# Cross-attention and FP4 feed-forward on one core: a step's small job put ahead of its maxima, rows' second half some steps later, another prologue

## The chip, the cores and the metric

The kernel runs on one core of one Trainium2 chip. The metric is the device time of one execution in microseconds (us). Engines are named as the profile does: PE (TensorE, its weight loads as PEld), DVE (VectorE), ACT (ScalarE), POOL (GpSimd) and SP (SyncE, which here only issues DMAs).

## The reference, cut to what matters

```python
# x: (8, 512, 256), ctx: (8, 1601, 256), 16 heads of 16
x = x + attention(layernorm(x), ctx, ctx)        # Wq, Wk, Wv, Wo with biases, softmax over 1601 keys
h = layernorm(x)
# fp4_quant_dequant: blocks of 16 along the last axis; scale = max|x| / 6; values to the grid 0, .5, 1, 1.5, 2, 3, 4, 6
gate = fp4(h) @ fp4(w_gate).T                    # 704 wide
up   = fp4(h) @ fp4(w_up).T
x = x + fp4(silu(gate) * up) @ fp4(w_down).T
```

## The kernel before, in words

The eight batches go through a software pipeline: a prologue ("pre"), then iterations "first", six times "loop", "last", and a "tail". An iteration computes the attention of one batch (part "att") and, in the same steps, the projections of the next batch ("early"), the feed-forward of the batch before ("late"), in "first" the rounding and transposing of the feed-forward weights ("once"), and the layernorm of the batch after the next ("next").

An iteration has 52 steps: 4 groups of 4 heads, 13 key tiles each. In a step PE computes two scores tiles (L811, `scores(n, 0)`), a job in a shared PSUM bank ("side 0": a piece of a projection, of gate, up or down), two more scores tiles, two products from which DVE takes row maxima for a later softmax (L828, `pair_products`; DVE reads them at L1082 and L1084), where the step has one a second, small job ("side 1"), and the weighted sum of the step before (L843). ACT takes the exponentials (L1007) and copies most jobs out of PSUM. All order is written out by hand: `SLOTS` says which jobs a step has on either side, `DVE_EXTRA` and `POOL_WORK` what DVE and POOL do besides.

In the loop all jobs use one bank, `misc`, in turn. So `shared(job)` first makes PE wait until the job before it was read. For a job of side 1 this is the job of side 0 in the same step: gate is read by ACT (tanh, L953) and DVE (L1111), up by DVE (L1116), a key piece by ACT (L938, L939), a value piece by ACT together with a context tile (L943, L919). Jobs of side 1 are transposes: `nm` (the maxima, L721), `hqT` (the hidden rows, L749), `xqT 1` (the second half of the rows, L732), and in "first" `ctx2` (context tiles, L681).

The rows that enter gate and up are rounded to FP4 in two halves: `xscale`, `xpower` and `xlast` on DVE, `xround` on POOL between the last two, then `xqT` on PE. The weights' pieces in "first" go through `W_AMAX_AT`, `W_SCALE_AT`, `W_SCALED_AT`, `W_POWER_AT`, `W_ROUND_AT` (steps on DVE and POOL) and end in `wT` (transposes on PE, two for each of six pieces; L768, L771). ACT loads the next piece after every second `wT`.

In the prologue `first_queries` has ACT issue the DMAs of the first group's queries and keys; then ACT waits until these have landed and issues the loads of the remaining weights (`weights_in`, L884 to L887). PE's sixth and seventh key pieces and the second query block (L692, L706) share three banks.

The side 1 transposes and the order that the change touches, in PE's loop over the steps:

```python
for job in products[between:2]:
    pair_products(job)
for job in jobs(it, n, 1):
    shared(job)
if n and has_att:
    weighted(n - 1, "att")
```

Of the kernel before, what the change touches and what calls it, by code (L numbers as in the profile page):

```python
# [12 lines left out]
I = 704  # L13
# [32 lines left out]
BLOCKS = 6 * 16  # L46
# [43 lines left out]
    16: ([("k", 5, "early")], []),  # L90
    17: ([("k", 6, "early")], []),
    18: ([("k", 7, "early")], []),
    19: ([("xqT", 0, "late")], [("xqT", 1, "late")]),
    20: ([("gate", 0, "late"), ("bob", 0, "once")], []),
    21: ([("gate", 1, "late"), ("wT", 0, "once")], [("nm", 2, "att")]),
    22: ([("up", 0, "late"), ("wT", 1, "once")], []),
    23: ([("up", 1, "late")], []),
    24: ([("gate", 2, "late"), ("wT", 2, "once")], []),
    25: ([("gate", 3, "late"), ("wT", 3, "once")], []),
    26: ([("up", 2, "late")], []),  # L100
    27: ([("up", 3, "late")], [("hqT", 0, "late")]),
    28: ([("gate", 4, "late")], [("hqT", 1, "late")]),
    29: ([("down0", 0, "late")], []),
    30: ([("down", 0, "late"), ("wT", 4, "once")], []),
    31: ([("gate", 5, "late"), ("wT", 5, "once")], []),
    32: ([("up", 4, "late")], [("hqT", 2, "late")]),
    33: ([("up", 5, "late")], [("hqT", 3, "late")]),
    34: ([("gate", 6, "late")], [("nm", 3, "att")]),
    35: ([("down0", 1, "late"), ("wT", 6, "once")], []),
    36: ([("down", 1, "late"), ("wT", 7, "once")], []),  # L110
    37: ([("gate", 7, "late")], [("hqT", 4, "late")]),
    38: ([("up", 6, "late")], [("hqT", 5, "late")]),
    39: ([("up", 7, "late")], []),
    40: ([("down0", 2, "late"), ("wT", 8, "once")], []),
# [43 lines left out]
for _step in SLOTS.values():  # L158
# [8 lines left out]
DVE_EXTRA = {  # L167
    2: [("late", "values", 4)], 3: [("late", "values", 5)], 4: [("late", "values", 6)], 5: [("late", "values", 7), ("late", "stats", 0)],
    7: [("late", "stats", 1), ("late", "mean", 0)], 8: [("late", "root", 0)], 9: [("late", "apply", 0)], 10: [("att", "nm", 1)],
    11: [("late", "xscale", 0)], 12: [("late", "xpower", 0)], 13: [("late", "apply", 1)], 14: [("late", "xscale", 1)], 15: [("late", "xpower", 1)],  # L170
    16: [("late", "xlast", 0)], 17: [("late", "xlast", 1)],
    21: [("att", "nm", 2)], 23: [("late", "hscale", 0)], 24: [("late", "hpower", 0)], 27: [("late", "hscale", 1)], 28: [("late", "hpower", 1)],
    29: [("att", "values", 0)], 30: [("att", "values", 1)], 32: [("att", "values", 2)], 33: [("late", "hscale", 2)], 34: [("late", "hpower", 2)], 36: [("att", "nm", 3)], 38: [("att", "values", 3)], 39: [("late", "hscale", 3)], 40: [("late", "hpower", 3)],
    43: [("next", "stats", 0)], 44: [("next", "stats", 1)], 45: [("next", "mean", 0)], 46: [("next", "root", 0)],
# [1 line left out]
}  # L176
PRE_EXTRA = {
    1: [("early", "stats", 0), ("early", "stats", 1), ("early", "mean", 0), ("early", "root", 0), ("early", "apply", 0), ("early", "apply", 1)],
    12: [("next", "stats", 0), ("next", "stats", 1)], 13: [("next", "mean", 0), ("next", "root", 0)], 14: [("next", "apply", 0), ("next", "apply", 1)],
    47: [("early", "nm", 0)],  # L180
}

TAIL_EXTRA = {
# [6 lines left out]
EXTRAS = {"pre": PRE_EXTRA, "first": DVE_EXTRA, "loop": DVE_EXTRA, "last": DVE_EXTRA, "tail": TAIL_EXTRA}  # L190


W_AMAX_AT = {12: 0, 14: 1, 24: 2, 27: 3, 33: 4, 39: 5}
W_SCALE_AT = {13: 0, 15: 1, 25: 2, 28: 3, 34: 4, 40: 5}
W_POWER_AT = {17: 0, 20: 1, 26: 2, 31: 3, 37: 4, 42: 5}
W_SCALED_AT = {14: 0, 16: 1, 25: 2, 28: 3, 34: 4, 40: 5}
W_ROUND_AT = {18: 0, 20: 1, 26: 2, 31: 3, 37: 4, 42: 5}
POOL_WORK = {
    0: [("late", "bias", 0)], 10: [("early", "k", 0)], 11: [("early", "k", 1)], 12: [("early", "q", 0), ("early", "k", 2)], 13: [("early", "k", 3)],
    14: [("late", "xround", 0), ("early", "k", 4)], 16: [("early", "q", 1), ("late", "xround", 1)], 17: [("early", "k", 5)], 18: [("early", "k", 6)], 19: [("early", "k", 7)],  # L200
    24: [("late", "hscaled", 0)], 25: [("late", "hround", 0)], 28: [("late", "hscaled", 1)], 29: [("late", "hround", 1)],
    34: [("late", "hscaled", 2)], 35: [("late", "hround", 2)], 40: [("late", "hscaled", 3)], 41: [("late", "hround", 3)],
}
# [68 lines left out]
def xattn_ffn(nc, x, ctx_in, wqT, wkT, wvT, woT, bq, bk, bv, bo, w_gate, w_up, w_down, out, scr_k, scr_q):  # L272
    es = ExitStack()
    with es:
# [38 lines left out]
        att = sb("att", [128, NC2, S])  # L313
# [5 lines left out]
        ht = sb("ht", [128, QT, I])  # L319

        mt = sb("mt", [128, QT * E])
        xnT = mt[:, :].rearrange("p (c n) -> p c n", c=NC2)
        hqT = sb("hqT", [128, NF, 128])
# [37 lines left out]
        k_stack = [[sem(f"k_stack{g}_{n}") for n in ("lead", "rest")] for g in range(NG)]  # L361
        q_stack = [[sem(f"q_stack{g}_{n}") for n in ("lead", "rest")] for g in range(NG)]
# [21 lines left out]
        def jobs(it, n, side):  # L384
            return [j for j in slots(it.kind, n)[side] if j[2] in it.parts]
# [28 lines left out]
        def maxima(it, n):  # L414

            part, first, number = ("early", 2 * (n - STEPS + M_LEAD), 2) if n >= STEPS - M_LEAD else ("att", 2 * (n + M_LEAD), 2)
            if it.kind == "first" and n < CATCH_UP:
                first, number = M_GROUP + AHEAD + 3 * n, 3
            if it.kind == "pre":

                first, last = (first, M_GROUP) if n < STEPS - M_LEAD + M_HEADS else (first - 2, M_GROUP + AHEAD)
                if not (n != STEPS - M_LEAD + M_HEADS and first < last):
                    return []
            if part not in it.parts:
                return []
            found = []
            for q in range(first, first + number):
                g, j = divmod(q, M_GROUP)
                pair, piece = divmod(j, M_HEADS)
                found.append((part, q, g, j, 2 * pair, piece))  # L430
            return found
# [4 lines left out]

        def rows_rounding(it, k):

            return mt[:, 0:512] if it.kind == "tail" else ht[:, :, :].rearrange("p t n -> p (t n)")[:, 512 * k:512 * (k + 1)]

        def raw_piece(p):

# [188 lines left out]
        def _(pe):  # L631
# [7 lines left out]
            def body(it):  # L639
# [209 lines left out]
                for n in range(STEPS):  # L849
                    if has_att:  # L850
                        scores(n, 0)
                    for job in jobs(it, n, 0):
                        shared(job)
                    products = maxima(it, n)

                    between = 1 if has_att and not jobs(it, n, 0) else 0
                    for job in products[:between]:
                        pair_products(job)
                    if has_att:
                        scores(n, 1)  # L860
                    for job in products[between:2]:
                        pair_products(job)
                    for job in jobs(it, n, 1):
                        shared(job)
                    if n and has_att:
                        weighted(n - 1, "att")
                    elif n == 0 and has_late:
                        weighted(STEPS - 1, "late")
                    for job in products[2:]:
                        pair_products(job)  # L870
# [3 lines left out]
        def _(act):  # L874
# [22 lines left out]
            def body(it):  # L897
# [123 lines left out]
                for n in range(STEPS):  # L1021
                    if has_att:
                        exps(n, 0)
                    for job in jobs(it, n, 0):
                        take(job)
                    if it.kind == "pre" and n == 14:
                        first_queries()
                        act.wait_ge(q_stack[0][1], BLOCKS)
                        act.wait_ge(k_stack[0][1], BLOCKS)
                        weights_in()  # L1030
                    if it.kind == "first" and n == 4:
                        raw_in(0)
                        raw_in(1)
                    if has_att:
                        exps(n, 1)
                    for job in jobs(it, n, 1):
                        take(job)
                    if n == 0 and has_late:
                        group_out(NG - 1, "late")
                    elif n and n % NKT == 0 and has_att:  # L1040
                        group_out(n // NKT - 1, "att")
# [4 lines left out]
        def _(dve):  # L1046
# [13 lines left out]
            def body(it):  # L1060
# [213 lines left out]
                for n in range(STEPS):  # L1274
                    for job in jobs(it, n, 0):
                        take(job)
                    if it.kind == "pre" and n == 11:
                        for piece in range(4):
                            first_keys(piece)
                    todo = maxima(it, n)  # L1280
                    for job in todo:
                        maximum(job)
                    for job in jobs(it, n, 1):
                        take(job)
                    if it.kind == "first":
                        if n in W_AMAX_AT:
                            weight_maxima(W_AMAX_AT[n])
                        if n in W_SCALE_AT:
                            weight_scales(W_SCALE_AT[n])
                        if n in W_POWER_AT:  # L1290
                            weight_powers(W_POWER_AT[n])
                    for part, what, k in EXTRAS[it.kind].get(n, []):
                        if part in it.parts:
                            extra(part, what, k)
# [5 lines left out]
        def _(pool):  # L1300
# [43 lines left out]
            def body(it):  # L1344
# [63 lines left out]
                for n in range(STEPS):  # L1408
# [10 lines left out]
                    if it.kind == "first":  # L1419
                        if n in W_SCALED_AT:  # L1420
                            weight_scaled(W_SCALED_AT[n])
# [31 lines left out]
```

## Time and profile before

| | |
|---|---|
| time, median of 3 runs (lowest, highest) | 1744.49 us (1743.31, 1746.17) |
| the profiled execution's own time | 1745.13 us |
| its span, first to last instruction | 1743.3 us |
| busy, share of the span: PE, DVE, ACT, POOL | 95%, 82%, 65%, 32% |
| mean granted TensorE clock, share of 2.4 GHz | 0.984 |

A timeline row gives start, duration, engine, line and operation, what is written and read, and in brackets how long the engine had been idle before it and what ended that. Consecutive groups of matmuls overlap a little in these rows, since their ends are modelled. Where a releaser named in brackets had ended long before, it was another that ended last.

### The profile page before, as it was taken

To read this page: it belongs to the slowest core of one execution; us is meant where nothing else is said; L and a number is where in the kernel's file an instruction comes from. 1 tells how busy PE (TensorE), PEld (TensorE's weight loads), DVE (VectorE), ACT (ScalarE), POOL (GpSimd) and SP (SyncE) were. 2 spreads that over 40 slices of the span, in tenths; PEclk is the share of its full clock that TensorE was granted. 3 is DMA by queue.
4 is the path that set the end of the run, shared out by engine and by line. 5 is a ranking of instruction groups with operands and counts; after the bars stand their busy time and mean duration, and the time that the engine had idled before them with its cause. 6 is when DMAs were issued, how large, how long until landed. Compare 5 with 4: busy or idle time off the path is not lost.

```text
span 1743.3 us, 26971 instructions
## 1 busy us (share of the span) xinstructions
PE 1648.1 (95%) x9408; PEld 656.0 (38%) x9408; DVE 1428.3 (82%) x2077; ACT 1131.4 (65%) x2293; POOL 564.2 (32%) x673
## 2 busy tenths in 40 slices
PE   5799899999999999999999999999999999989958
PEld 2332234333433344333443334333443334323325
DVE  6777988988788978988889887889879887889347
ACT  2377677766777667776677667776677766666731
POOL 4328520732025330443107321263304431013304
PEclk8899999999999999999999999999999999999979
DMA  5645332331234333142323322244222322200000
GB/s 162 145 85 123 88 69 44 85 105 38 56 58 107 83 60 57 51 112 48 78 45 83 102 41 58 46 117 85 58 54 54 77 47 66 44 7 10 13 22 13
DMA packets 106770, 117.52 MB, mean 67 GB/s; under 512 B 23236, under 2 KB 88140, under 8 KB 106636
## 3 DMA queue, kind: packets, MB, share of 16 engines
q1 hardware_dynamic: 101808, 111.62, 30.0%
q10 hardware_dynamic: 4828, 4.18, 1.0%
q8 instruction: 75, 1.23, 0.3%
q14 instruction: 59, 0.48, 0.1%
HBM read 76.78 MB, written 30.16 MB: 61 GB/s over the span
## 4 chain that ended last, share of the span: by engine, by line
PE 74%; DVE 15%; ACT 4%; POOL 3%; issue 2%; DMA 1%; SPq 1%; ACTq 0%; POOLq 0%; DVEq 0%
PE pvb L843 19%; PE st L811 18%; PE mx L828 9%; PE misc L741 7%; DVE cmx L1082 7%; PE misc L713 5%; PE misc L706 3%; PE misc L761 3%; ACT prob L1007 3%; PE misc L753 2%; PE misc L692 1%; PE misc L727 1%; PE misc L749 1%; POOL ht L1333 1%; PE misc L782 1%
## 5 line engine op out<-in xcount | busy, mean ns | idle before, releaser
L1007 ACT ACTIVATE prob<-st 128x512 f32<-128x512 f32 (+1 forms) x1590 | 867.2, 599 | 378.7 <-PE st L811 376.2
L1082 DVE TENSOR_REDUCE cmx<-mx 128x2 f32<-128x1024 f32 x768 | 905.8, 1220 | 156.4 <-PE mx L828 153.0
L811 PE MATMUL st<-qstack,kstack 112*128 112x512 bf16 (+1 forms) x1590 | 497.0, 385 | 9.9 <-ACT prob L1007 4.2
L843 PE MATMUL pvb<-prob,vv 128*32 128x512 f32 (+1 forms) x3328 | 444.7, 606 | 0.5 <-ACT prob L1007 0.5
L811 PEld LDWEIGHTS st<-qstack,kstack 112*128 112x128 bf16 (+1 forms) x1590 | 127.6, 98 | 463.4 <-issue 239.9
L828 PE MATMUL mx<-kstack,qstack 48*128 48x512 bf16 (+1 forms) x2048 | 257.9, 338 | 31.1 <-DVE cmx L1082 22.6
L1341 POOL TENSOR_TENSOR ht<-ht,rh 128x352 f32<-128x352 f32 (+1 forms) x78 | 56.8, 751 | 439.2 <-DVE rh L1058 439.2
L741 PE MATMUL misc<-wguT,rowsT 128*128 128x352 f32 x456 | 153.7, 459 | 0.0
L1333 POOL TENSOR_TENSOR ht<-ht,mt 128x352 f32<-128x352 f32 (+1 forms) x140 | 124.4, 911 | 73.5 <-DVE mt L1239 60.8
L828 PEld LDWEIGHTS mx<-kstack,qstack 48*128 48x128 bf16 x2048 | 59.4, 94 | 214.6 <-issue 131.7
L1347 POOL TENSOR_TENSOR cin<-cin 128x400 f32<-128x400 f32 (+1 forms) x60 | 55.8, 931 | 239.2 <-ACT cin L939 239.2
L843 PEld LDWEIGHTS pvb<-prob,vv 128*32 128x32 f32 (+1 forms) x3328 | 65.7, 108 | 133.4 <-issue 121.5
L1364 POOL TENSOR_TENSOR x<-x,bob 128x256 f32<-128x256 f32 x32 | 22.3, 729 | 287.0 <-issue 270.9
L741 PEld LDWEIGHTS misc<-wguT,rowsT 128*128 128x128 f32 x456 | 86.5, 190 | 40.9
L713 PE MATMUL misc<-wv,ctxT 128*128 128x256 f32 (+1 forms) x392 | 101.8, 382 | 0.0
L706 PE MATMUL misc<-ctxT,wk 128*128 128x400 f32 (+1 forms) x236 | 91.5, 510 | 0.0
L713 PEld LDWEIGHTS misc<-wv,ctxT 128*128 128x128 f32 (+1 forms) x392 | 73.1, 187 | 21.2 <-issue 0.5
L1144 DVE RECIPROCAL sums<-sums 128x128 f32<-128x128 f32 x64 | 60.3, 942 | 17.7 <-DMA sums<-pvs 17.7
L1341 POOL TENSOR_TENSOR ht<-ht,sh 128x352 f32<-128x352 f32 (+1 forms) x82 | 62.4, 783 | 2.9
L1333 POOL TENSOR_TENSOR xa<-xa,ht 128x256 f32<-128x256 f32 x56 | 43.1, 790 | 54.9 <-DVE ht L1196 53.8
L1351 POOL TENSOR_TENSOR cin<-cin 128x400 bf16<-128x400 f32 (+1 forms) x60 | 58.2, 970 | 4.7
L938 ACT ACTIVATE cin<-misc,bqk 128x400 f32<-128x400 f32 (+1 forms) x59 | 35.1, 595 | 32.8 <-PE misc L706 30.5
(182 smaller groups left out, 1542.0 us busy)
## 6 DMA issues: line engine op xcount, KB each, us to landing
kstack<-scr_k SPq DMA_DIRECT2D x378, 100.1 KB, 4.3
scr_k<-cin SPq DMA_DIRECT2D x48, 300.0 KB, 3.9
qstack<-scr_q SPq DMA_DIRECT2D x372, 32.0 KB, 1.8
cin<-ctx_in SPq DMA_DIRECT2D x16, 512.0 KB, 5.3
scr_q<-qp SPq DMA_DIRECT2D x16, 384.0 KB, 4.2
scr_k<-cin SPq DMA_DIRECT2D x16, 300.8 KB, 4.9
xn<-x SPq DMA_DIRECT2D x8, 512.0 KB, 3.9
cin<-ctx_in SPq DMA_DIRECT2D x16, 256.0 KB, 5.4
```

The costliest lines, as they stand in the source:

```text
L706: last = mm(o[:, 0:w], wk[:, h, m * 128:(m + 1) * 128], ctxT[:, h, COFF[n]:COFF[n] + w], start=(h == 0), stop=(h == NC2 - 1))
L713: last = mm(o[0:w, 0:E], ctxT[:, h, KOFF[j]:KOFF[j] + w], wv[:, h, :], start=(h == 0), stop=(h == NC2 - 1))
L741: last = mm(o[:, 0:IH], rowsT[:, h, t * 128:(t + 1) * 128], wguT[:, h, first:first + IH], start=(h == 0), stop=(h == NC2 - 1))
L811: mm(score_bank(it, n, h)[0:KROWS[kt], :], kstack[:, hd, KOFF[kt]:KOFF[kt] + KROWS[kt]], qstack[:, hd, :], start=True, stop=True).then_inc ...
L828: last = mm(mx[:, q % 2, par, at:at + w], qstack[r0:r0 + LEAD, hd, t * 128:(t + 1) * 128], kstack[r0:r0 + LEAD, hd, k0:k0 + w], start=True ...
L843: last = mm(pvb[2 * D * h:2 * D * (h + 1), :], vv[0:w, kt, (HG * g + h) // 2, D * (h % 2):D * (h % 2 + 2)], prob[0:w, n % 2, h, :], start= ...
L1007: activate(prob[0:KROWS[kt], n % 2, 2 * pair + h, :], score_bank(it, n, 2 * pair + h)[0:KROWS[kt], :], ACT.Exp, scale=SCALE).then_inc(exp_ ...
L1082: v.tensor_reduce(cmx[:, g % 2, h0:h0 + 2, at:at + 1], products, op=ALU.max, axis=AX.X).then_inc(max_free, 1)
L1144: v.reciprocal(sums[:, cols], sums[:, cols]).then_inc(rec_ready, 1)
L1333: last = g_.tensor_tensor(out[:, cols], in0[:, cols], in1[:, cols], op)
L1341: last = g_.tensor_tensor(part, part, over(sc[:, j * w:(j + 1) * w]), ALU.mult)
L1351: g_.tensor_tensor(parts[:, 2, :], whole, parts[:, 1, :], ALU.subtract).then_inc(done, 1)
```

## The change

The second half of the rows moves back: `xscale 1` from step 14 to 15, `xpower 1` from 15 to 17, `xlast 1` from 17 to 20, `xround 1` on POOL from step 16 (ahead of key pieces 5 and 6) to 18 (behind them), `xqT 1` from step 19 to 22; its scratch lies at another place in `ht`. In "first", `wT` 0 to 7 and most of their preparation come a step or two later. In the prologue half of a layernorm's last operation goes from step 14 to 50, and ACT no longer waits for the stacks before `weights_in`, which goes to step 36. On PE a step's side 1 job is put ahead of its products, and on DVE the side 1 job ahead of the maxima.

```diff
-    19: ([("xqT", 0, "late")], [("xqT", 1, "late")]),
+    19: ([("xqT", 0, "late")], []),
-    21: ([("gate", 1, "late"), ("wT", 0, "once")], [("nm", 2, "att")]),
-    22: ([("up", 0, "late"), ("wT", 1, "once")], []),
-    23: ([("up", 1, "late")], []),
-    24: ([("gate", 2, "late"), ("wT", 2, "once")], []),
-    25: ([("gate", 3, "late"), ("wT", 3, "once")], []),
-    26: ([("up", 2, "late")], []),
+    21: ([("gate", 1, "late")], [("nm", 2, "att")]),
+    22: ([("up", 0, "late"), ("wT", 0, "once")], [("xqT", 1, "late")]),
+    23: ([("up", 1, "late"), ("wT", 1, "once")], []),
+    24: ([("gate", 2, "late")], []),
+    25: ([("gate", 3, "late"), ("wT", 2, "once")], []),
+    26: ([("up", 2, "late"), ("wT", 3, "once")], []),
...
-    30: ([("down", 0, "late"), ("wT", 4, "once")], []),
-    31: ([("gate", 5, "late"), ("wT", 5, "once")], []),
-    32: ([("up", 4, "late")], [("hqT", 2, "late")]),
+    30: ([("down", 0, "late")], []),
+    31: ([("gate", 5, "late"), ("wT", 4, "once")], []),
+    32: ([("up", 4, "late"), ("wT", 5, "once")], [("hqT", 2, "late")]),
...
-    35: ([("down0", 1, "late"), ("wT", 6, "once")], []),
-    36: ([("down", 1, "late"), ("wT", 7, "once")], []),
-    37: ([("gate", 7, "late")], [("hqT", 4, "late")]),
+    35: ([("down0", 1, "late")], []),
+    36: ([("down", 1, "late"), ("wT", 6, "once")], []),
+    37: ([("gate", 7, "late"), ("wT", 7, "once")], [("hqT", 4, "late")]),
...
-    11: [("late", "xscale", 0)], 12: [("late", "xpower", 0)], 13: [("late", "apply", 1)], 14: [("late", "xscale", 1)], 15: [("late", "xpower", 1)],
-    16: [("late", "xlast", 0)], 17: [("late", "xlast", 1)],
+    11: [("late", "xscale", 0)], 12: [("late", "xpower", 0)], 13: [("late", "apply", 1)], 15: [("late", "xscale", 1)], 16: [("late", "xlast", 0)],
+    17: [("late", "xpower", 1)], 20: [("late", "xlast", 1)],
...
-    12: [("next", "stats", 0), ("next", "stats", 1)], 13: [("next", "mean", 0), ("next", "root", 0)], 14: [("next", "apply", 0), ("next", "apply", 1)],
-    47: [("early", "nm", 0)],
+    12: [("next", "stats", 0), ("next", "stats", 1)], 13: [("next", "mean", 0), ("next", "root", 0)], 14: [("next", "apply", 0)],
+    47: [("early", "nm", 0)], 50: [("next", "apply", 1)],
...
-W_AMAX_AT = {12: 0, 14: 1, 24: 2, 27: 3, 33: 4, 39: 5}
-W_SCALE_AT = {13: 0, 15: 1, 25: 2, 28: 3, 34: 4, 40: 5}
-W_POWER_AT = {17: 0, 20: 1, 26: 2, 31: 3, 37: 4, 42: 5}
-W_SCALED_AT = {14: 0, 16: 1, 25: 2, 28: 3, 34: 4, 40: 5}
-W_ROUND_AT = {18: 0, 20: 1, 26: 2, 31: 3, 37: 4, 42: 5}
+W_AMAX_AT = {12: 0, 14: 1, 25: 2, 28: 3, 34: 4, 39: 5}
+W_SCALE_AT = {13: 0, 15: 1, 26: 2, 31: 3, 35: 4, 40: 5}
+W_POWER_AT = {17: 0, 20: 1, 27: 2, 33: 3, 37: 4, 42: 5}
+W_SCALED_AT = {14: 0, 16: 1, 26: 2, 31: 3, 35: 4, 40: 5}
+W_ROUND_AT = {18: 0, 20: 1, 27: 2, 33: 3, 37: 4, 42: 5}
...
-    14: [("late", "xround", 0), ("early", "k", 4)], 16: [("early", "q", 1), ("late", "xround", 1)], 17: [("early", "k", 5)], 18: [("early", "k", 6)], 19: [("early", "k", 7)],
+    14: [("late", "xround", 0), ("early", "k", 4)], 16: [("early", "q", 1)], 17: [("early", "k", 5)], 18: [("early", "k", 6), ("late", "xround", 1)], 19: [("early", "k", 7)],
...
-            return mt[:, 0:512] if it.kind == "tail" else ht[:, :, :].rearrange("p t n -> p (t n)")[:, 512 * k:512 * (k + 1)]
+            return mt[:, 0:512] if it.kind == "tail" else ht[:, :, :].rearrange("p t n -> p (t n)")[:, 2 * I * k:2 * I * k + 512]
...
+                    for job in jobs(it, n, 1):
+                        shared(job)
                     for job in products[between:2]:
                         pair_products(job)
-                    for job in jobs(it, n, 1):
-                        shared(job)
...
                         first_queries()
-                        act.wait_ge(q_stack[0][1], BLOCKS)
-                        act.wait_ge(k_stack[0][1], BLOCKS)
+                    if it.kind == "pre" and n == 36:
                         weights_in()
...
-                    todo = maxima(it, n)
-                    for job in todo:
-                        maximum(job)
                     for job in jobs(it, n, 1):
                         take(job)
+                    for job in maxima(it, n):
+                        maximum(job)
```

## Rows read from the trace of the kernel before

**Rows 1.** Stretches: length; busy PE, PEld, DVE, ACT, POOL; granted clock; DMA.
```profile
881.49:1085.32 203.83, 200.69 (x1174) 80.37 (x1171) 173.92 (x253) 140.90 (x286) 64.68 (x74) 1.00 0.33 70
1541.00:1544.40 3.40, 2.37 (x26) 0.54 (x21) 3.37 (x5) 2.52 (x5) 2.64 (x4) 0.95 0.08 19
1544.40:1547.30 2.90, 2.90 (x14) 0.39 (x12) 2.87 (x5) 0.51 (x2) 0.18 (x1) 0.50 0.22 51
```

**Rows 2.** Waits of PE in that loop iteration: total us, times, longest.
```profile
PE mx L828 <- DVE cmx L1082: 1.0, 2, 0.8
PE st L811 <- ACT prob L1007: 0.5, 1, 0.5
PE misc L721 <- DVE ht L1111: 0.4, 2, 0.2
PE misc L749 <- DVE ht L1111: 0.4, 2, 0.2
PE misc L721 <- ACT cin L939: 0.2, 1, 0.2
```

**Rows 3.** Timeline of PE in step 34 of that iteration.
```profile
1017.04 0.60 PE L811 MATMUL st<-qstack,kstack 112*128 112x512 bf16 x2
1017.57 0.60 PE L828 MATMUL mx<-kstack,qstack 48*128 48x512 bf16 x4
1018.38 0.28 PE L721 MATMUL misc<-ident,nmx 128*16 128x128 f32 x1 [0.21 <-DVE ht L1111]
1018.59 1.07 PE L843 MATMUL pvb<-prob,vv 128*32 128x512 f32 x8
```

**Rows 4.** Timeline of PE in step 34 of "last", which has no products.
```profile
1620.41 0.28 PE L721 MATMUL misc<-ident,nmx 128*16 128x128 f32 x1 [0.74 <-DVE ht L1111]
1620.62 1.06 PE L843 MATMUL pvb<-prob,vv 128*32 128x512 f32 x8
```

**Rows 5.** Timeline of steps 32 to 34 of the loop iteration, PE and DVE.
```profile
1009.00 0.53 DVE L1116 SCALAR_TENSOR_TENSOR ht<-misc,ht 128x352 f32<-128x352 f32 x1 [0.31 <-PE misc L741]
1009.32 0.61 PE L828 MATMUL mx<-kstack,qstack 48*128 48x512 bf16 x4
1009.86 0.66 PE L749 MATMUL misc<-ident,ht 128*128 128x128 f32 x4
...
1012.03 0.94 DVE L1144 RECIPROCAL sums<-sums 128x128 f32<-128x128 f32 x1
...
1013.27 0.52 DVE L1116 SCALAR_TENSOR_TENSOR ht<-misc,ht 128x352 f32<-128x352 f32 x1
...
1014.04 0.44 PE L749 MATMUL misc<-ident,ht 128*128 128x128 f32 x2
1017.81 0.52 DVE L1111 SCALAR_TENSOR_TENSOR ht<-xn,misc 128x352 f32<-128x352 f32 x1
```

**Rows 6.** Timeline of step 43: the copy that frees the bank, the products.
```profile
1053.25 0.38 ACT L919 COPY ctxT<-misc 128x256 f32<-128x256 f32 x1
1053.26 0.61 PE L828 MATMUL mx<-kstack,qstack 48*128 48x512 bf16 x4
```

**Rows 7.** Timeline of steps 17 to 19: POOL's rounding, ACT's key piece, PE.
```profile
948.53 3.37 POOL L1333 TENSOR_TENSOR xa<-xa,ht 128x256 f32<-128x256 f32 x4 [0.82 <-DVE ht L1196]
953.82 1.22 POOL L1351 TENSOR_TENSOR cin<-cin 128x400 bf16<-128x400 f32 x1
955.12 0.60 ACT L938 ACTIVATE cin<-misc,bqk 128x400 f32<-128x400 f32 x1 [1.21 <-PE misc L706]
```

**Rows 8.** Timeline of the prologue.
```profile
43.21 0.69 ACT L927 ACTIVATE qx<-st,bqk 128x512 f32<-128x512 f32 x1 [17.65 <-issue]
44.53 1.99 PE L706 MATMUL st<-ctxT,wk 128*128 128x400 f32 x4 [3.62 <-ACT qp L928]
47.10 1.23 DVE L1082 TENSOR_REDUCE cmx<-mx 128x2 f32<-128x1024 f32 x1 [4.17 <-PE mx L828]
```

**Rows 9.** Timeline of PE at step 21 of "first".
```profile
161.44 0.61 PE L768 MATMUL misc<-ident,ht 88*128 88x88 f32 x4 [1.79 <-POOL ht L1341]
```

## The prediction

> **What bounds the kernel now.** I read the page first (its totals stand in the table), then the stretches, PE's waits, and the timeline around each edited step. The first thing to see is that one loop iteration takes 203.83 us, of which PE is busy 200.69 at the full clock [rows 1]; the five other loop iterations, laid out by the starts of their steps, agree within 0.1. DVE has 30 us to spare there, ACT 63. PE's list of waits is short: 1.0 us for maxima, 0.5 for exponentials, and at five places about 0.2 before a small transpose [rows 2]. So each 0.1 us by which PE stands longer in a loop step comes back six times in the sum, and work of DVE, ACT or POOL counts only where PE would wait for it.
>
> The second thing is what these five waits look like. In step 34 the four products start 0.07 before the scores are modelled to end, take 0.60, and only then PE waits, 0.21 us, for DVE's read of gate, which frees the bank [rows 3]. The wait before `nm` is much longer; the products lie in it. "last" shows it without them, since there no later batch needs maxima: the same transpose waits 0.74 [rows 4]. The weighted sum behind it stands in PE's queue, although its exponentials are of the step before: PE waits in order.
>
> **PE's order.** The edit adds no instruction. It puts the products behind the transpose, and so behind its wait. A transpose starts 0.05 after the release: gate's read ends at 1017.81 + 0.52 = 1018.33 [rows 5], the transpose starts at 1018.38 [rows 3]. I price each place in a loop iteration by when the bank is freed against when PE gets there.
>
> (a) Steps 10, 21, 28, 34 and 37, the five of [rows 2], where PE waits even behind the products: their whole time, 0.60 less the overlap of 0.07, is no longer hidden. 5 x 0.53 = 2.65.
>
> (b) Steps 27, 32, 33 and 38, a transpose behind up, and step 22, where `xqT 1` comes to stand behind up 0. In step 32 DVE's read ends at 1009.00 + 0.53 = 1009.53, so the transpose can start at 1009.58; PE's place for it, where the products start now, is 1009.32 [rows 5]. PE stands 0.25. 5 x 0.25 = 1.25.
>
> (c) Steps 43, 44 and 47, behind a value piece and its context tile: ACT's copy ends at 1053.25 + 0.38 = 1053.63, plus 0.05, against 1053.26 [rows 6]. 3 x 0.42 = 1.26.
>
> (d) Late next is DVE. Its maxima now start later by the transposes too, 0.66 - 0.07 = 0.59 for four of them and 0.44 - 0.07 = 0.37 for two [rows 5]. Mostly DVE's idle time takes that up. It does not where DVE runs without a gap up to the read that frees the next bank: in step 33 up is read at 1013.27, as the work begun at 1012.03 ends [rows 5], so step 33 stands 0.59 longer; step 34 follows step 33's two transposes in the same way, 0.37. In step 22 DVE splits the maxima of `nm 2` just before it reads up 0; I take 0.3, between 0 and 0.59. Sum 1.26; bounds 0 and some 3 (0.59 at two more places and in step 22).
>
> Together 6.42 us per loop iteration. DVE's half of this edit does nothing: of the side 1 kinds DVE takes only up and down, which stand there in the tail alone, and the tail has no maxima.
>
> **Rows' second half.** Its DVE work keeps its durations. In steps 15 to 17 PE waits for nothing from DVE, so lighter steps there give nothing; PE's 1.0 us for maxima [rows 2] falls in steps 13 and 14, before the first moved operation. POOL is different: `xround 1` takes 3.37 us ahead of key piece 5 [rows 7]. ACT's copy of piece 7 starts at 955.12, just after POOL finished piece 5 at 953.82 + 1.22 = 955.04 (PE, which the row names, had ended a microsecond before); ACT's exponentials come late, and PE waits 0.5 for them at step 19's first scores [rows 2]. With the rounding behind piece 6 this goes, with the overlap -0.52 per iteration; bounds -0.52 and 0, as `xpower 1`, now in step 17, may hold step 19's products 0.0 to 0.35. `xlast 1` in step 20 falls into idle time of DVE. `xqT 1` costs PE its 0.59 in step 22 instead of step 19: zero. Keys leave POOL some 1.5 us later, behind which SP next waits for `nm 2` anyway, so its queue is not late. The other scratch address costs nothing.
>
> So the loop: 6 x (6.42 - 0.52) = +35.4.
>
> **"last".** Products end at step 33 there. Steps 21, 22, 27, 28, 32, 33 cost 0.53 + 0.55 + 0.25 + 0.53 + 0.25 + 0.84 = 2.95, step 34 0.37 from DVE's lateness. Between steps 9 and 18 DVE is the bound in this iteration, and one `xlast` of 0.7 leaves that stretch: -0.7. Sum +2.6, bounds +1 and +4.
>
> **"first".** `ctx2` in steps 1 to 3 stands as in (c), 1.26, step 10 0.53, step 47 0.42: +2.2. The weights: `wT 0` waits 1.79 us for POOL in step 21 [rows 9]; a step later POOL is done, -1.8. Against it piece 3 is scaled three steps later and rounded two steps later, its transposes come one step later, so some 2.5 us of POOL's lead there are lost; half of that seems to be taken up by waits that shrink at other pieces. I take -1.0 for the weights, bounds -3 and +2.5. Sum +1.2.
>
> **Prologue.** ACT, free of own work for 17.65 us, copies the second query block only at 43.21, behind its waits and DMA issues; PE's key piece waits 3.62 us for the bank that this frees, and DVE's maxima, the chain that ends the prologue, stand 4.17 us [rows 8]. Without the waits ACT copies some 9 us earlier, before PE asks for the bank. The weights' loads are issued about 1 us later; their first user may wait a little. I take -3.8, bounds -4.2 and -2. The half `apply` at step 50 falls into DVE's wait for the first scores: zero; without that cover it costs under 1.
>
> **Sum.** 35.4 + 2.6 + 1.2 - 3.8 = +35.4 on the profiled execution's 1745.13, or 1780.5; that run lies 0.64 above the median of the runs shown, so 1780 us.
>
> **Rivals.** *The clock.* PE stands more often. In "last", after a stretch in which PE was busy 2.37 of 3.40 us, the granted clock was 0.50 for some 2.9 us [rows 1], its lower level of 1.2 GHz. Against it: step 14's waits of 1.0 us in all leave the clock at 1.00 in the loop [rows 1, 2]. In step 34 the wait would be 0.74 + 0.37 = 1.1 us. The Trainium skill (TensorE: Matmul & The Clock Gate, "HAM oscillation — how this bites in real kernels") shows a clock lost to waits for DMAs between bursts, longer than any here; by that alone the sum would stay, and the trace already disagrees, with the 0.50 above. Once per loop iteration and in "last", half of about 3 us: 7 x 1.5 = +10, 1790; at three places each, +31, 1812.
>
> *DVE's lateness costs nothing*, because its idle time takes it up everywhere: without (d), 1780 - 6 x 1.26 - 1.2 = 1771.
>
> *Faster: PE does not hold the products behind a waiting transpose.* If the queue let them pass, (a) to (d) would be nothing and the moves of POOL and the prologue would be left: -6 x 0.52 - 3.8 - 1 - 0.7, about 1736. It decides from the point at which the order's price falls below some 1 us per loop iteration, a sixth of mine. Against it stands the weighted sum held in [rows 4]. The Trainium skill (the same page, "Step-by-step: what each phase is for") says that only weight loads are pulled ahead and matmuls stay in order; the trace agrees, with the 0.74.
>
> *Half of it.* Releases come earlier in a way I do not see, and PE stands half as long: 1760.
>
> **How the numbers follow.** Forecast with or without (d) 0.68, the clock 0.17, half 0.09, faster 0.04, and 0.02 for an amount of no change, in which gains and waits cancel. 0.2% (3.5 us) is about what a measurement can tell from no change. The range: down to 1767, the case without (d) with the bounds of the weights; up to 1799, with step 19's stall (+2), the weights (+3.5), (d) at its bound (+10), or the clock lost once or twice. It leaves out half and faster below, the clock lost often above. Slower 0.94, same 0.02, faster 0.04.
>
> **What would show it.** In the profile after, a loop iteration of about 209.7 us; PE's waits before L721, L749 and L732 near 0.7 us in (a), 0.2 in (b), 0.8 and 1.1 in steps 33 and 34, 0.35 in (c); L828 never between scores and a side 1 transpose; ACT's wait before piece 7 0.4 instead of 1.21; the first scores near 71.4 instead of 75.23. Wrong it would be if these waits are not there, if PE's clock falls inside loop iterations, or if the weights in "first" hold PE by several microseconds at `wT 6`.

## The result, and the profile after

| | before | changed |
|---|---|---|
| time, median (lowest, highest), same chip | 1744.91 us | 1788.04 us (1786.51, 1789.41) |
| ratio, 95% interval | | 1.0244 [1.0231, 1.0257] |
| span of the profiled execution | 1743.3 us | 1784.7 us |
| busy, share of the span: PE, DVE, ACT, POOL | 95%, 82%, 65%, 32% | 93%, 80%, 63%, 31% |

The changed kernel is 2.4% slower; the forecast was 1780 us, with a range of 1767 to 1799. Laid out by the starts of each step's first scores, the span's +41.4 us divides like this:

| part | forecast | measured |
|---|---|---|
| prologue, up to the first scores | -3.8 | -3.73 (71.50 instead of 75.23) |
| "first" | +1.2 | +7.8 |
| six loop iterations | +35.4 | +35.5 (five of +6.1 to +6.3, the sixth +4.7) |
| "last" | +2.6 | +2.0 |
| tail | 0 | -0.2 |

The loop iteration that answers to the first row of [rows 1], from the same view of stretches:

```profile
904.08:1114.09 210.01, 201.30 (x1174) 80.45 (x1171) 174.22 (x253) 140.86 (x286) 63.63 (x74) 1.00 0.32 68
```

The instructions are the same in number; PE is busy 201.30 us instead of 200.69, but the iteration is 6.2 us longer. So PE stands, at the full clock. Where it stands, the waits of PE in that stretch say, beside [rows 2]:

```profile
PE misc L721 <- DVE ht L1110: 1.8, 2, 1.1
PE misc L749 <- DVE ht L1110: 1.5, 2, 0.7
PE misc L749 <- DVE ht L1115: 1.3, 4, 0.7
PE mx L828 <- DVE cmx L1081: 1.0, 2, 0.8
PE misc L721 <- ACT cin L939: 0.7, 1, 0.7
PE misc L732 <- DVE ht L1115: 0.5, 1, 0.5
PE misc L749 <- ACT ctxT L919: 0.4, 1, 0.4
PE misc L749 <- ACT vv L943: 0.4, 1, 0.4
PE misc L721 <- ACT vv L943: 0.4, 1, 0.4
```

(DVE's lines have numbers one lower than before.) The 0.5 for exponentials is gone, and ACT's wait before key piece 7 is 0.41, the 0.4 of the forecast; the run with the rows alone, below, puts that down to the rows. Every line but that for maxima is a side 1 transpose waiting for its bank. The five short waits of before are now near 0.7, or 1.1 in step 34, and eight places are new. Step 34, PE's timeline, against [rows 3]:

```profile
1042.77 0.60 PE L811 MATMUL st<-qstack,kstack 112*128 112x512 bf16 x2
1044.44 0.28 PE L721 MATMUL misc<-ident,nmx 128*16 128x128 f32 x1 [1.07 <-DVE ht L1110]
1044.65 0.61 PE L828 MATMUL mx<-kstack,qstack 48*128 48x512 bf16 x4
1045.19 0.64 PE L843 MATMUL pvb<-prob,vv 128*32 128x512 f32 x4
```

The products, which need neither the bank nor gate, come 0.21 us after the transpose's start instead of lying under its wait. DVE's timeline of the same step shows why the bank is free so late:

```profile
1041.27 0.69 DVE L1083 TENSOR_REDUCE cmx<-mx 128x8 f32<-128x520 f32 x1
1042.00 0.22 DVE L1087 TENSOR_REDUCE nmx<-cmx 128x16 f32<-128x64 f32 x1
1042.14 0.88 DVE L1218 TENSOR_REDUCE ah<-ht 128x44 f32<-128x704 f32 x1
...
1043.75 0.20 DVE L1057 SCALAR_TENSOR_TENSOR rh<-rh 128x44 f32<-128x44 f32 x1
1043.87 0.51 DVE L1110 SCALAR_TENSOR_TENSOR ht<-xn,misc 128x352 f32<-128x352 f32 x1
```

DVE goes from the maxima to the read of gate without a gap; its maxima began later, since the products did.

The prologue, ACT, PE and DVE, against [rows 8]:

```profile
34.02 0.69 ACT L927 ACTIVATE qx<-st,bqk 128x512 f32<-128x512 f32 x1 [8.04 <-issue]
38.23 2.03 PE L706 MATMUL st<-ctxT,wk 128*128 128x400 f32 x4
40.63 7.07 DVE L1081 TENSOR_REDUCE cmx<-mx 128x2 f32<-128x1024 f32 x6 [0.35 <-PE mx L828]
```

ACT copies the second query block 9.2 us earlier, PE's key piece finds its bank free, and DVE's 4.17 us gap is 0.35.

In "first" the time was lost at two places: steps 0 to 3, of whose loss the forecast had half, and the weights, which it had with the wrong sign. PE's timeline, steps 0 and 1, then 23, then 36:

```profile
78.28 0.39 PE L828 MATMUL mx<-kstack,qstack 48*128 48x512 bf16 x2 [1.11 <-DVE cmx L1081]
...
81.12 0.63 PE L681 MATMUL misc<-ident,cin 128*128 128x128 f32 x4 [0.41 <-ACT vv L943]
...
168.84 0.61 PE L828 MATMUL mx<-kstack,qstack 48*128 48x512 bf16 x2 [0.74 <-DVE cmx L1081]
...
216.40 0.64 PE L768 MATMUL misc<-ident,ht 88*128 88x88 f32 x4 [4.04 <-POOL ht L1339]
```

The last is `wT 6`; POOL, in the same stretch, began the piece only when DVE's power (L1271, at 207.42) came:

```profile
208.19 5.63 POOL L1331 TENSOR_TENSOR ht<-ht,rowsT 88x256 f32<-88x256 f32 x8 [4.41 <-DVE rowsT L1271]
213.90 2.35 POOL L1339 TENSOR_TENSOR ht<-ht,sh 88x256 f32<-88x256 f32 x4
```

Behind the waits of 0.74 and 4.04 the clock fell, as the stretches around them show (the third number from the end is the granted clock, a mean over its two levels):

```profile
166.51:171.31 4.80, 3.64 (x16) 0.67 (x16) 4.54 (x5) 2.00 (x5) 4.64 (x8) 0.74 0.54 161
214.00:219.00 5.00, 2.60 (x14) 0.95 (x18) 1.07 (x3) 1.51 (x3) 3.74 (x6) 0.76 0.00 0
```

### The profile page after: what moved, and what is told of

Its sections match the earlier page's. It is cut to its first block, busy times and chain, and to the rows that moved or that the text cites. A ratio compares the mean times of both kernels' runs of the same rounds, so it can differ in the third digit from the quotient of the medians.

```text
span 1784.7 us, 26970 instructions
## 1 busy us (share of the span) xinstructions
PE 1651.0 (93%) x9408; PEld 656.6 (37%) x9408; DVE 1427.8 (80%) x2077; ACT 1131.0 (63%) x2293; POOL 557.5 (31%) x673
## 4 chain that ended last, share of the span: by engine, by line
PE 70%; DVE 20%; ACT 4%; issue 3%; POOL 1%; DMA 1%; ACTq 0%; SPq 0%; POOLq 0%; DVEq 0%
PE pvb L843 18%; PE st L811 16%; PE mx L828 10%; DVE cmx L1081 9%; PE misc L741 6%; PE misc L713 5%; PE misc L706 3%; PE misc L761 3%; ACT prob L1007 2%; PE misc L753 2%; PE misc L749 2%; PE misc L692 1%; PE misc L727 1%; DVE ht L1115 1%; PE misc L782 1%
## 5 line engine op out<-in xcount | busy, mean ns | idle before, releaser
L1143 DVE RECIPROCAL sums<-sums 128x128 f32<-128x128 f32 x64 | 60.4, 943 | 17.5 <-DMA sums<-pvs 17.4
L1083 DVE TENSOR_REDUCE cmx<-mx 128x8 f32<-128x520 f32 x64 | 44.5, 695 | 15.7 <-PE mx L828 15.5
```

The source lines that it names most:

```text
L1143: v.reciprocal(sums[:, cols], sums[:, cols]).then_inc(rec_ready, 1)
```

## The experiments

The theory is the forecast's: PE takes its queue in order, and a transpose that waits for its bank now holds the products. The rivals: the order is cheap and the cost sits in the moved work of DVE and POOL; DVE's lateness is not part of it; the cost comes from the order as such, not from the wait. The first four runs take each part of the change alone, the others undo or shift one thing or put parts together. The edits of the first four concern different jobs, and with DVE's half of the order edit they make up the whole diff.

**The order alone.** On the kernel before:

```diff
-                    for job in products[between:2]:
-                        pair_products(job)
                     for job in jobs(it, n, 1):
                         shared(job)
+                    for job in products[between:2]:
+                        pair_products(job)
```

> The kernel before with nothing changed but the place of the side 1 jobs ahead of the products in TensorE's order. Theory (TensorE takes its queue in order, so a transpose that waits for its bank also holds the products that used to lie under that wait): what the trace of the changed kernel shows in the steps with a side 1 job behind gate, up and value pieces, 0.25 to 0.87 us each, is all there; 34 us in the six loop iterations, 2.7 in last, some 4 in first, 41 together, and up to 4 more if xqT 1 waits in step 19 as well: 1786 to 1790 us. Rival (the cost comes from the moved DVE and POOL work, the order costs half or less): at most 1766. Rival (products pass the waiting transpose): 1745.

Measured: 1788.15 us against 1746.33, ratio 1.0242 [1.0228, 1.0256], span 1784.3. The six loop iterations give +35.2, "first" +3.6, "last" +2.8. One loop iteration, in the view of stretches:

```profile
903.44:1113.37 209.93, 201.19 (x1175) 80.32 (x1171) 172.98 (x253) 140.75 (x286) 64.67 (x74) 1.00 0.32 68
```

So the order by itself makes the whole slowdown, and both rivals with small prices fall. `xqT 1`, here still in step 19, costs 0.15 there. The run also tells wait and order apart. "first" has no gate before `nm 2` and `nm 3`, their bank is free, and PE starts both without a wait: with the same new order, steps 21 and 34 of "first" are as long as before, within 0.03 us. PE's timeline there, step 21 and then 34 (no bracket, so no wait):

```profile
165.68 0.42 PE L721 MATMUL misc<-ident,nmx 128*16 128x128 f32 x1
...
211.82 0.27 PE L721 MATMUL misc<-ident,nmx 128*16 128x128 f32 x1
```

It is the wait that costs.

**The prologue alone.** On the kernel before:

```diff
                         first_queries()
-                        act.wait_ge(q_stack[0][1], BLOCKS)
-                        act.wait_ge(k_stack[0][1], BLOCKS)
+                    if it.kind == "pre" and n == 36:
                         weights_in()
...
-    14: [("next", "apply", 0), ("next", "apply", 1)],
-    47: [("early", "nm", 0)],
+    14: [("next", "apply", 0)],
+    47: [("early", "nm", 0)], 50: [("next", "apply", 1)],
```

> The kernel before with the prologue's edits alone: ScalarE's two waits and the weights' loads taken from step 14, the loads issued at step 36, half of apply at step 50. Theory: the first scores start near 71.5 us instead of 75.2 and nothing is given back: 1741.2 us (-3.7). Rival: the late loads are what makes the context transposes of first's steps 1 to 3 cost 2.8 us in the changed kernel instead of the 1.3 forecast, so 1.6 is given back there: 1742.8 us, and those steps are longer than before by some 0.5 us each.

Measured: 1740.67 against 1746.33, ratio 0.9969 [0.9957, 0.9981]; span 1739.4, so -3.9. The first scores start at 71.14; steps 0 to 3 of "first" are unchanged within 0.01, so the rival falls. The half of `apply` that was moved runs from 72.19 to 72.91, and DVE's next maxima still wait 2.81 for PE: zero, as forecast. Step 50 of "first" is 0.17 longer here and in every kernel with this prologue; ACT begins its exponentials there after 0.94 of idle instead of 0.67, and why stays open.

**Rows' second half alone.** On the kernel before, the `SLOTS`, `DVE_EXTRA`, `POOL_WORK` and `rows_rounding` lines that concern it:

```diff
-    ...14: [("late", "xscale", 1)], 15: [("late", "xpower", 1)], 16: [("late", "xlast", 0)], 17: [("late", "xlast", 1)],
+    ...15: [("late", "xscale", 1)], 16: [("late", "xlast", 0)], 17: [("late", "xpower", 1)], 20: [("late", "xlast", 1)],
-    16: [("early", "q", 1), ("late", "xround", 1)], 17: [("early", "k", 5)], 18: [("early", "k", 6)],
+    16: [("early", "q", 1)], 17: [("early", "k", 5)], 18: [("early", "k", 6), ("late", "xround", 1)],
```

> The kernel before with the rows' second half moved alone (xqT 1 from step 19 to 22, VectorE's and GpSimd's operations for it, the scratch address). Theory: GpSimd's rounding no longer stands ahead of key piece 5, -0.55 us in step 18 of each loop iteration, against +0.18 in step 17 for the power now there; -2.0 in last, where the clock's drop after step 14 goes: 6 x -0.37 - 2.0 = -4.2, 1740.7 us. Rival (xqT 1 behind up 0 waits in step 22 under the old order too, some 0.2 each): 1742 us. Rival (the moves only shift work): 1744.9.

Measured: 1741.83 against 1746.33, ratio 0.9978 [0.9969, 0.9987], span -3.2. Per loop iteration -0.34: step 17 +0.18, step 18 -0.55, and `xqT 1` moves its 0.59 from step 19 to 22 without more. "last" gives -0.8 rather than -2.0: its clock does not fall here at step 14 (-0.97), but step 6 loses 0.36, and of `xqT 1`'s 0.59, paid in step 22, step 19 gives back only 0.29. The first theory holds for the loop; its sum was -4.2, by the spans -3.2, by the medians -4.5.

**The weights alone.** On the kernel before, the `wT` jobs and the five `W_` tables as in the change.

> The kernel before with the weights' transposes of first and their VectorE and GpSimd work moved alone; the loop and last are then those of before. Theory: TensorE waits some 4 us in front of wT 6, whose piece GpSimd rounds only after VectorE's power at step 33, and then loses the clock; 1.8 us are gained at wT 0: 1747 to 1749 us. Rival (the forecast's -1.0; the stall comes only with TensorE's order, which makes VectorE late): 1743.9 us.

Measured: 1749.56 against 1746.33, ratio 1.0020 [1.0011, 1.0029], span +3.5, of which +2.3 lies in "first": -3.05 in step 21, +1.61 in step 23, +4.85 in step 36, the rest small. The wait at `wT 6` is there under the old order, to the hundredth as in the changed kernel:

```profile
215.69 0.50 PE L768 MATMUL misc<-ident,ht 88*128 88x88 f32 x4 [4.04 <-POOL ht L1341]
```

So it is made by the tables: the power of piece 3 was put two steps later, and POOL's 8 us of rounding start from it.

The four spans differ by +41.0, -3.9, -3.2 and +3.5, together +37.4; the whole change has +41.4. Some 3 us of the rest is `xqT 1`: it costs 0.58 in step 22 when both its move and the order are there, against 0.15 in step 19 with the order alone, in seven iterations. About 1.3 lies in "first". These are spans of single executions; the medians give +41.8, -5.7, -4.5 and +3.2, together +34.9 against +43.1, each uncertain by 1.6 to 2.4, so they settle only that the order is nearly all of it.

**The whole change with the products first again.**

```diff
+                    for job in products[between:2]:
+                        pair_products(job)
                     for job in jobs(it, n, 1):
                         shared(job)
-                    for job in products[between:2]:
-                        pair_products(job)
```

> The changed kernel with one thing undone: the products again ahead of the side 1 jobs in TensorE's order. Theory (the order costs 41.5 us by itself, and 0.43 us per iteration more through xqT 1, which in the changed kernel stands in step 22 behind up 0 and takes the products' cover away there): 1788 less 44 to 46, so 1742 to 1744 us, a little under the kernel before, and the loop iteration 203.5 us. Rival (the parts have costs of their own that the order only makes visible): above 1750 us.

Measured: 1741.4 against 1744.88, ratio 0.9979 [0.9970, 0.9988]; a loop iteration takes 203.50. Everything but the order makes the kernel a little faster. DVE's half of the order edit is still in this kernel and in no step shows a cost.

**DVE's lateness.** On the changed kernel:

```diff
-    32: [("att", "values", 2)], 33: [("late", "hscale", 2)], 34: [("late", "hpower", 2)],
+    33: [("late", "hscale", 2)], 34: [("late", "hpower", 2)], 35: [("att", "values", 2)],
```

> The changed kernel with VectorE's values 2 (0.94 + 0.29 us) moved from step 32 to step 35, so that it no longer stands in front of the read of up that frees the bank in step 33. Theory (VectorE's lateness, term (d)): step 33 stands 0.25 us longer than before the change instead of 0.77, so -0.52 in each of seven iterations: about 1784.4 us. Rival (the transposes of step 33 cost what they cost, or the work comes back in step 35 or 36): 1788 us.

Measured: 1782.6 against 1744.88, ratio 1.0220 [1.0203, 1.0237]. Step 33 is 0.25 longer than before instead of 0.77, in all seven iterations, and no other step of the loop changes; "first" gives 1.6 more. In PE's waits of a loop iteration, L749's longest behind up falls from 0.7 to 0.2:

```profile
PE misc L749 <- DVE ht L1115: 0.7, 4, 0.2
```

The rival falls, and the part of (d) in step 33 is shown.

**Weight piece 3 earlier.** On the changed kernel:

```diff
-W_SCALE_AT = {13: 0, 15: 1, 26: 2, 31: 3, 35: 4, 40: 5}
-W_POWER_AT = {17: 0, 20: 1, 27: 2, 33: 3, 37: 4, 42: 5}
+W_SCALE_AT = {13: 0, 15: 1, 26: 2, 29: 3, 35: 4, 40: 5}
+W_POWER_AT = {17: 0, 20: 1, 27: 2, 31: 3, 37: 4, 42: 5}
```

(`W_SCALED_AT` and `W_ROUND_AT` likewise.)

> The changed kernel with weight piece 3 scaled at step 29 instead of 31 and rounded at step 31 instead of 33 (VectorE's and GpSimd's parts of it); the transposes stay where they are. Theory: GpSimd is done before wT 6, its 4.0 us wait and the clock's fall behind it go: -5 us, 1783 us, and the loop unchanged. Rival (GpSimd has no room at step 31 and holds rows' rounding or another piece): 1786 us or more.

Measured: 1784.69 against 1744.88, ratio 1.0226 [1.0212, 1.0240], between theory and rival. Against the changed kernel step 36 is 5.13 us shorter, as expected, and step 23, which the edit does not touch, 1.1; but step 31 is 1.2 longer and step 40 2.1 longer. In step 40 `wT 8` waits as long as in the changed kernel, and here the clock falls with it (226.52), there it does not (231.65), by the lengths of the transposes. PE's timeline of this kernel, then of the changed kernel:

```profile
226.52 1.09 PE L771 MATMUL misc<-ident,ht 128*128 128x128 f32 x4 [1.30 <-POOL ht L1339]
```

```profile
231.65 0.63 PE L771 MATMUL misc<-ident,ht 128*128 128x128 f32 x4 [1.31 <-POOL ht L1339]
```

In step 23 it is the other way round: the wait of 0.74 is the same as in the changed kernel, but here the clock stays at 1.00. PE's row, and the stretch of step 23, 4.54 us instead of 5.64:

```profile
168.90 0.39 PE L828 MATMUL mx<-kstack,qstack 48*128 48x512 bf16 x2 [0.74 <-DVE cmx L1081]
...
165.67:170.21 4.54, 3.40 (x24) 1.09 (x21) 4.51 (x6) 2.42 (x5) 4.38 (x8) 1.00 0.46 134
```

**The parts that gain.** The kernel before with the prologue's edits, the weights with piece 3 early, and of the rows' edits only `xround 1`, `xlast 1` and `xqT 1`; scale and power stay in steps 14 and 15.

> The kernel before, in its own order on TensorE, with those parts of the change that gain: the prologue (-2.8 us by the trace of its own run), GpSimd's rounding behind key piece 6 with the last part of rows' second half in step 20 and xqT 1 in step 22, but scale and power left where they were (-0.55 in each of six iterations, -3.3), and the weights' transposes moved with piece 3 early (-3, from +2.3 less 5). Theory: the parts add, -9 us: ratio 0.995 to the kernel before. Rival (first and last lose the clock at other places, and half goes): 0.9975.

Measured: 1741.29 against 1744.88, ratio 0.9973 [0.9964, 0.9982]. The rival's number, and its reason in part. The span is 3.9 shorter where the theory has 9. "first", where the weights were to gain 3, is 0.4 longer in all: steps 31 and 40 are 1.2 and 1.6 longer than before, and in step 40 the clock falls (0.71 over the step). What the rival did not name is that the loop gains 0.8 instead of 3.3, for step 17 of each iteration is 0.39 longer. Its timeline, DVE and then PE:

```profile
942.42 1.27 DVE L1194 TENSOR_SCALAR ht<-xa 128x512 int32<-128x512 int32 x1
943.72 1.05 DVE L1195 TENSOR_SCALAR ht<-ht 128x512 f32<-128x512 f32 x1
944.70 2.34 DVE L1081 TENSOR_REDUCE cmx<-mx 128x2 f32<-128x1024 f32 x2
...
947.10 0.39 PE L828 MATMUL mx<-kstack,qstack 48*128 48x512 bf16 x2 [0.21 <-DVE cmx L1081]
```

L1195 takes 0.43 where POOL rests. With the rounding gone from there POOL starts the next key piece at once, and DVE's power runs beside it; the maxima start late, and PE's second pair of products waits for them.

**Scale where it was.** The same, with one more line:

```diff
-14: [("late", "xscale", 1)], 15: [("late", "xpower", 1)], 16: [("late", "xlast", 0)], 20: [("late", "xlast", 1)],
+14: [("late", "xscale", 1)], 16: [("late", "xlast", 0)], 17: [("late", "xpower", 1)], 20: [("late", "xlast", 1)],
```

> e8_parts_that_gain with one difference: the scale of rows' second half stays in step 14, its power goes to step 17 as in the changed kernel. In e8 step 17 of the loop stands 0.39 us longer than before, as VectorE's second power operation took 1.06 us instead of 0.43 beside GpSimd's key piece; in the changed kernel it is 0.18, with the scale (1.16 instead of 0.27 us) in step 16. Theory (VectorE's operations on SBUF alone are held while GpSimd works): here the scale runs in step 15 beside an idle GpSimd in 0.27 us, step 17 costs nothing, the loop iteration is 203.3 us (-0.53), and the time some 2.4 us under e8: ratio 0.9960 to the kernel before. Rival (step 17 is late by the place of the power, or of the rounding, as such): loop iteration 203.5 or more, ratio 0.9973.

Measured: 1737.06 against 1744.84, ratio 0.9955 [0.9941, 0.9969]. Step 17 is as before within 0.01, step 18 0.52 shorter:

```profile
877.35:1080.69 203.34, 200.66 (x1174) 80.30 (x1171) 173.71 (x253) 140.96 (x286) 64.64 (x74) 1.00 0.32 70
```

DVE's two short operations of the scale in this kernel, as POOL ends a piece at 938.91 and then stands 0.83 us, and in the changed kernel, beside POOL's work on queries and keys:

```profile
938.69 0.27 DVE L1053 SCALAR_TENSOR_TENSOR sx<-ax,tiny 128x32 f32<-128x32 f32 x1
939.38 0.19 DVE L1057 SCALAR_TENSOR_TENSOR rx<-rx 128x32 f32<-128x32 f32 x1
```

```profile
969.41 1.16 DVE L1053 SCALAR_TENSOR_TENSOR sx<-ax,tiny 128x32 f32<-128x32 f32 x1
970.99 0.91 DVE L1057 SCALAR_TENSOR_TENSOR rx<-rx 128x32 f32<-128x32 f32 x1
```

POOL in the changed kernel at that time:

```profile
969.37 1.15 POOL L1349 TENSOR_TENSOR qp<-qx,qp 128x512 bf16<-128x512 f32 x1
970.90 0.95 POOL L1345 TENSOR_TENSOR cin<-cin 128x400 f32<-128x400 f32 x1 [0.38 <-ACT cin L939]
```

Each of DVE's two operations ends 0.05 us after the POOL instruction beside it: 970.57 after 970.52, 971.90 after 971.85. This is the fastest of all kernels run, ahead of both.

**Power of weight piece 1 later.** On the changed kernel, `W_POWER_AT` 20: 1 becomes 22: 1.

> The changed kernel with VectorE's power of weight piece 1 moved from step 20 to 22 in first, so that GpSimd, which waits for it, does not yet round that piece while VectorE splits the maxima of nm 2. Theory (GpSimd's work makes the split long): the four operations of the split take 0.97 us in all as elsewhere, instead of 2.66; TensorE's 0.74 us wait for maxima in step 23 and the clock's fall behind it go, step 23 is 2 to 3 us shorter; against it wT 2 in step 25 waits some 4 us for GpSimd, so the time is about that of the changed kernel, 1787 to 1790 us. Rival (the split is long for a reason of its own in that iteration): it stays at 2.7 us and step 23 at 5.6 us.

Measured: 1789.26 against 1744.84, ratio 1.0257 [1.0243, 1.0271]. The split of `nm 2`, DVE's timeline in the changed kernel and then here:

```profile
163.75 0.59 DVE L1131 CAST nmp<-nmf 16x128 bf16<-16x128 f32 x1
164.37 0.72 DVE L1132 TENSOR_TENSOR nmr<-nmf,nmp 16x128 f32<-16x128 f32 x1
165.13 0.64 DVE L1133 CAST nmp<-nmr 16x128 bf16<-16x128 f32 x1
165.80 0.72 DVE L1134 TENSOR_TENSOR nmp<-nmr,nmp 16x128 bf16<-16x128 f32 x1
```

```profile
161.64 0.20 DVE L1131 CAST nmp<-nmf 16x128 bf16<-16x128 f32 x1
161.88 0.89 DVE L1132 TENSOR_TENSOR nmr<-nmf,nmp 16x128 f32<-16x128 f32 x1
162.80 0.21 DVE L1133 CAST nmp<-nmr 16x128 bf16<-16x128 f32 x1
163.05 0.28 DVE L1134 TENSOR_TENSOR nmp<-nmr,nmp 16x128 bf16<-16x128 f32 x1
```

The sum is 1.58, not the 0.97 expected, because the second operation still ran beside the last instruction of a key piece (POOL 161.74 to 162.63); the other three have their usual lengths. Step 23 is 2.15 shorter, its wait for maxima and the clock's fall gone; `wT 2` waits 3.97 for POOL and the clock falls there. The theory holds, and the second operation agrees with it. But the split took 2.40 in the kernel before too, without a wait in step 23. There PE stood 1.79 at `wT 0` in step 21 and lost the clock, and so came to step 23 later; in all seven kernels with the moved weights and this power at step 20 the wait is 0.74. That the earlier arrival brings the wait out is read from these rows, and not tested by itself.

## Why the prediction was right, and where it was not

**PE's order: right, term by term.** (a) 0.54 at each place against 0.53; (b) 0.25 to 0.26 against 0.25; (c) 0.43 to 0.48 against 0.42. The order alone gave the whole ratio, so that products do not pass a waiting transpose is shown, and with it what the Trainium skill (TensorE: Matmul & The Clock Gate, "Step-by-step: what each phase is for") says of matmuls staying in order.

**(d), DVE's lateness: right.** Steps 33, 34 and 22 have 0.52, 0.33 and 0.33 beyond (a) and (b), against 0.59, 0.37 and 0.3. Only step 33's was tested by itself. The loop's sum agrees more closely than its parts: a typical iteration has +6.17 against 5.90, and in the sixth, where value pieces have no context tile behind them, (c) is missing, which the forecast counted six times (it read the loop iterations as equal within 0.1; the sixth took 203.08 before the change, the others 203.8 to 203.9).

**Rows' second half: the gain right (-0.55 against -0.52), one premise wrong.** "Its DVE work keeps its durations" failed. The scale, one step later, runs beside a key piece and takes 1.6 us longer, so step 17 loses 0.18; the forecast looked for such a loss in step 19, from the power, and took zero. The Trainium skill (SBUF — State Buffer, "SBUF: two separate sides") says that DVE operations with two SBUF inputs or in a two-port mode and GpSimd instructions exclude each other for a whole instruction. The traces agree: 0.27 and 1.16 for the same operation in the runs above.

**"first": the failed term, +7.8 against +1.2.** Of the four steps with `ctx2`, 0 was left out, and in steps 1 to 3 the 0.42 is there, but a third pair of products then waits some 0.2 for DVE, whose maxima start late behind the products; 2.8 instead of 1.26. The weights were the larger error: steps 21 to 39 give +3.7, beyond the upper bound of +2.5. With the weights alone these steps give +2.3; most of the difference is the clock, which falls in step 23 of the changed kernel and not in that run. The sign of the term was wrong either way. The sentence that failed is that half of POOL's lost lead "seems to be taken up by waits that shrink at other pieces". 4.04 us stand at `wT 6`, which the forecast had named as a sign of being wrong, and the clock falls there. It should have been followed through DVE's table: POOL cannot start before DVE's power, and that was put two steps later against one step for the transposes. At `wT 0` the gain was larger than the 1.8 forecast, 3.15 in step 21, for the clock's fall went with the wait, but half or more of it comes back in step 23.

**Prologue: right.** -3.73 against -3.8, by the mechanism forecast. The agreement to 0.1 is partly luck: in the eight kernels with this prologue the first scores start between 70.66 and 72.20.

**"last": right in size, partly by luck.** +2.0 against +2.6. Steps 21 to 34 give +3.9, where the forecast had 3.3 (`xqT 1`'s 0.59 is paid in step 22, and step 19 gives back only 0.28). Steps 9 to 19 give -1.8 instead of -0.7, as the clock's fall in step 14 did not come; the errors partly cancel.

**The clock rival fell in the loop:** 1.00 in spite of waits of 1.07 us. The forecast of 1780 lacked 8 us. By the spans it lacked 6, with 6.6 in "first" and -0.6 in "last"; most of the rest is that the profiled execution of the changed kernel is the fastest of its four. The range held, and its lower end is 2 us under what the terms named for it give (1771 less 2 for the weights).

## What to carry over

Before moving an instruction ahead of others on PE, which takes them in order, ask what it waits for: independent work placed in front hides the wait, placed behind it waits too, and so does the engine fed by that work. Price each place as release time minus arrival time, then look one engine further for who becomes late; that gave the loop here to 0.3 us in 6. When work is moved in time, its duration is a term as well: check what POOL does beside DVE in the new place, and follow the whole chain of producers, not only the last one.

## What the runs showed of the hardware

Some DVE operations on SBUF take several times as long when POOL is at work: the scale's L1053 0.27 or 1.16 us, L1057 0.19 or 0.91, the split's casts 0.20 or 0.6, its subtraction 0.28 or 0.72 to 0.89. Others do not: the scale's maxima from SBUF (L1187) take 0.68, the reciprocal of the sums (L1143) 0.94, and maxima from PSUM 1.22 either way. And it goes both ways: where DVE's L1215 (0.68) starts just ahead of POOL's L1350 (945.50 and 945.59 in the fastest kernel), POOL's instruction takes 1.34 instead of 0.89.

Whether the clock falls behind a wait is not told by the wait's length alone. At the same instruction it fell after 0.74 us in the changed kernel and not in the run with piece 3 earlier (step 23); after 1.30 in that run and not after 1.31 in the changed kernel (step 40); after 1.79 in the kernel before and not after 1.80 in the run with the rows alone (`wT 0`). It never fell after the 1.07 of the loop iterations. A fall costs about 1.1 us in step 23 (5.64 against 4.54). What decides stays open here; so a change that removes a wait in "first" may have its gain taken back by a fall some steps on, as with piece 3, and a microsecond or two in "first" and in "last" is not the edit's doing for certain.
